# The last batch of an attention and expert kernel, written out for each engine in another order

## The chip, the cores and the metric

One core of a Trainium2 chip runs the kernel. The metric is the device time of one execution in microseconds (us), the median of several runs. The profile lists every instruction of one execution, in us from the first instruction. TensorE has two clock levels, 1.2 and 2.4 GHz; the profile gives the granted clock as a share of the higher one.

## The reference, cut to what matters

For each of four batches of 512 tokens with 128 features: 16-head attention, a layer norm with gamma and beta, a residual and a second layer norm; then a layer that picks 4 of 32 experts for each token, a residual and a third norm.

```python
x = _layernorm(x + _L0_attn_ref(x, Wq, Wk, Wv, rel_table, gamma, beta))   # inside: norm "a"; outside: norm "b"
x = _layernorm(x + _L0_ffn_ref(x, hasher_w, keys, values_down, values_up, scale))          # norm "c"
# _L0_ffn_ref:
h = einsum('btd,pd->btp', x, hasher_w); sim = einsum('btp,np->btn', h, keys)
vals, idx = top_k(sim, 4); w = softmax(vals)
for k in range(4):
    proj = silu(einsum('btd,btdp->btp', x, values_down[idx[..., k]]))
    out = out + einsum('btp,btpd->btd', proj, values_up[idx[..., k]]) * w[..., k:k+1]
return x + out * scale
```

## The kernel before

The kernel runs in rounds `t` of 16 units `u`; each unit has attention scores, exponentials and value products of four heads and a 128-key chunk (`scores`, `exp`, `values`). Round `t` also does the norms, top-4 and first expert layer of batch `t-1`, and the second layer of batch `t-2`. Tables (`JOBS`) say at which unit which small job of TensorE stands; every engine has its own program, written in this order, and semaphores tie them together. After the four attention rounds comes a fifth, `TAIL` (`t == B`), which has no attention, and behind it some lines for the last batch alone. The last batch is `f = B - 1`. A 512-token batch lies as four chunks `c` of 128 tokens.

For that last batch the order of the work is this. The attention output is turned (L1057) and divided on VectorE; `tail_norms` adds the bias, takes statistics and mean (L799, L808), waits for GpSimd to make the inverse root (L432), and scales (L831); gamma, residual and norm "b" follow in the same way. Between them VectorE does the third norm's statistics of batch 2 (`late_y`, L936), whose second-layer products (L1073) run on TensorE meanwhile. `x1` is turned on TensorE, copied by ScalarE to `x1_t`, and the similarities `sim` are made (L1122), copied by ScalarE and searched by VectorE (L885 to L924), with `sdiff` on GpSimd (L550) and the exponential on ScalarE (L728), which also has the tanh of the first layer. The first layer (L1137) makes eight 128x512 products `down0` to `down7`, one for four experts, in three PSUM banks in turn: a bank is free when VectorE's `hidden` (L823) has read it. GpSimd splits the weights in three bf16 parts (L454 to L460), TensorE turns them (`wt`) and ScalarE copies them. `spread_weights` (L1142) then spreads the weights of four experts over a bank of 128x512; VectorE multiplies six of the eight `hid` tiles by it (L967), GpSimd two (L446), from a copy by ScalarE. Only when all eight spreads are done do the eight second-layer products `up0` to `up7` begin (L1073, eight matmuls each in the trace). VectorE adds the residual, takes statistics (L799, L808), GpSimd the inverse root, VectorE scales four chunks (L977), and SyncE stores 256 KB.

PSUM has eight banks: `st_ps` (3), `sm_ps` (2), `ov_ps`, `mi_ps` and `si_ps`. In the attention rounds all have a use; in the tail `st_ps` has the first layer, and `sm_ps`, `ov_ps`, `mi_ps` the spreads.

Of the kernel before, what the change touches and what calls it, by code (L numbers as in the profile page):

```python
# [5 lines left out]
def bass_postln_attention_product_key_ffn(nc, x, w_q, w_k, w_v, rel_table, gamma, beta,  # L6
# [6 lines left out]
    B, S, E = x.shape  # L13
# [4 lines left out]
    J = 4  # L18
# [29 lines left out]
    with ctx:  # L48
# [97 lines left out]
        tail_made, late_step, late_pool = sem("tail_made"), sem("late_step"), sem("late_pool")  # L146
        weighed, tail_weighed = sem("weighed"), sem("tail_weighed")
# [15 lines left out]
        SHORT_JOBS = {**JOBS, 5: ([], []), 6: (["x1t", "shift2"], ["sim", "down0"])}  # L163
        OWN = ("shift0", "shift1", "shift2", "shift3", "o0")
# [26 lines left out]
        def jobs_at(kind, u):  # L191

            return (SHORT_JOBS if kind == SECOND else JOBS).get(u, ([], []))
# [21 lines left out]
        TAIL_VECTOR = [j for j in range(FJ) if j % 3 != 2]  # L215
        TAIL_POOL = [j for j in range(FJ) if j % 3 == 2]

        def hidden_count(f, j):
            return f * FJ + (j + 1)

        def down_bank(t, j):
# [30 lines left out]
        POOL_TAIL, LATE_POOL_TAIL = ["aeps", "apow", "beps", "bpow", "sdiff"], ["ceps", "cpow"]  # L252

        def pool_at(f, name):
            tail = f == B - 1
            if name in LATE_POOL:
                return f * len(LATE_POOL) + ((LATE_POOL_TAIL if tail else LATE_POOL).index(name) + 1)
            return f * len(POOL_STEPS) + ((POOL_TAIL if tail else POOL_STEPS).index(name) + 1)

        def act_at(f, name):  # L260
            return f * len(ACT_STEPS) + (ACT_STEPS.index(name) + 1)
# [22 lines left out]
        def rounds(engine, round_):  # L284

            for t, kind in enumerate(KINDS):
                round_(t, *kind)

# [3 lines left out]
        def _(sp):  # L292
# [96 lines left out]
            store(B - 1)  # L389
            sp.wait_ge(y_stored, 16 * B + 1)  # L390

        @block.gpsimd
        def _(pool):
# [121 lines left out]
            def round_(t, attention, experts, more, late):  # L515
# [11 lines left out]
                if experts and not attention:  # L527
                    norm(f, "a", EPS_ATTENTION, None, None, centre=False)
                    norm(f, "b", EPS_LN, None, None, centre=False)
                    late_norm(t - 2)  # L530
                elif experts:
# [24 lines left out]
                if experts:  # L556
                    split_weights(f)
                    for j in range(FJ // 2) if attention else TAIL_POOL:
# [731 lines left out]
```

## Time and profile before

| | us |
|---|---|
| median of 3 runs (lowest, highest) | 338.67 (338.07, 338.92) |
| the profiled execution's own time | 337.84 |
| its span, first to last instruction | 336.0 |
| TensorE busy in the span | 300.0 |
| last attention output ready in PSUM (end of L1051) | 288.15 |

The last row says where the tail begins: 47.85 us of the span lie behind the last attention product. Outside the span there is 1.84 us. In a row of the timeline the two first numbers are the start and the length, both in us, then come engine, line, operation, what is written and read, shape, how many instructions were merged, and in brackets how long the engine had been idle and what released it. In a row of stretches come start and end, the length, the busy us (and instructions) of TensorE's matmuls, its weight loads, VectorE, ScalarE and GpSimd, the granted clock as a share of 2.4 GHz, the DMA share and GB/s.

### The profile page before, as it was taken

How to read it: one execution, taken by the hardware profiler on the slowest of the kernel's cores; microseconds unless marked ns; L12 is line 12 of the kernel's file. 1: busy time of each engine (PE TensorE's matmuls, PEld its weight loads, DVE VectorE, ACT ScalarE, POOL GpSimd, SP SyncE). 2: the span in 40 equal slices, each digit the busy share in tenths (PEclk: the TensorE clock that was granted, in tenths of full speed). 3: DMA queues.
4: the chain of work that ended last, by engine and by line, in shares of the span. 5: the costliest groups of instructions: out<-in, count | busy, mean ns of one | idle time of the engine just before them, and what ended most of it. 6: DMA issues, size and time to landing. Idle time of an engine off the chain costs nothing. (4 is left out here: it accounts for less than half of the span.)

```text
span 336.0 us, 4908 instructions
## 1 busy us (share of the span) xinstructions
PE 300.0 (89%) x1639; PEld 124.1 (37%) x1639; DVE 235.6 (70%) x514; ACT 200.9 (60%) x392; POOL 126.1 (38%) x208
## 2 busy tenths in 40 slices
PE   4878889999999899999999999999989999837890
PEld 2544322232222233334552433335624232634380
DVE  4448687878879779877659898786598721375533
ACT  2674475776767577787546777884457799202400
POOL 8491700110017502273267212742663237223121
PEclk9999999999999999999999999999999999996797
DMA  5495693099230220102011210120001000001001
GB/s 159 105 271 141 169 295 99 13 324 315 67 72 17 55 57 20 51 21 71 1 36 38 67 40 30 44 60 14 1 0 36 1 1 2 0 0 31 2 0 31
DMA packets 28230, 23.17 MB, mean 69 GB/s; under 512 B 6526, under 2 KB 26670, under 8 KB 28206
## 3 DMA queue, kind: packets, MB, share of 16 engines
q1 hardware_dynamic: 28206, 22.87, 25.0%
q8 instruction: 13, 0.21, 0.3%
q14 instruction: 11, 0.09, 0.1%
HBM read 12.18 MB, written 10.52 MB: 68 GB/s over the span
## 5 line engine op out<-in xcount | busy, mean ns | idle before, releaser
L769 DVE TENSOR_REDUCE neg_max<-sm_ps 128x1 f32<-128x512 f32 x256 | 167.6, 684 | 43.8 <-PE sm_ps L1026 42.9
L668 ACT ACTIVATE probs<-st_ps 128x512 f32<-128x512 f32 x256 | 138.1, 612 | 47.9 <-PE st_ps L1037 47.6
L1026 PE MATMUL sm_ps<-k_stack,q_stack 96*128 96x512 bf16 x256 | 98.1, 384 | 7.7 <-DVE neg_max L769 5.2
L1037 PE MATMUL st_ps<-q_stack,k_stack 128*128 128x512 bf16 x256 | 86.4, 380 | 1.9 <-ACT probs L668 0.8
L1051 PE MATMUL ov_ps<-probs,v_cur 128*32 128x512 f32 x512 | 68.2, 605 | 0.5 <-ACT probs L668 0.5
L1026 PEld LDWEIGHTS sm_ps<-k_stack,q_stack 96*128 96x128 bf16 x256 | 24.6, 96 | 100.7 <-DVE neg_max L769 82.8
L446 POOL TENSOR_TENSOR hid<-hid,w_rows 128x512 f32<-128x512 f32 x26 | 33.1, 1275 | 41.2 <-ACT w_rows L579 34.3
L1037 PEld LDWEIGHTS st_ps<-q_stack,k_stack 128*128 128x128 bf16 x256 | 25.2, 99 | 29.1 <-ACT probs L668 9.3
L1073 PEld LDWEIGHTS si_ps<-up_sb,hid 128*128 128x128 f32 x256 | 30.6, 192 | 1.0
L1073 PE MATMUL si_ps<-up_sb,hid 128*128 128x128 f32 x256 | 31.0, 275 | 0.0
L1137 PE MATMUL mi_ps<-x_t,down_sb 128*128 128x512 f32 x48 | 25.1, 604 | 0.3 <-ACT shift_rows L579 0.3
L823 DVE SCALAR_TENSOR_TENSOR hid<-tanh_sb,mi_ps 128x512 f32<-128x512 f32 x24 | 16.3, 679 | 11.8 <-ACT tanh_sb L705 11.8
L705 ACT ACTIVATE tanh_sb<-mi_ps 128x512 f32<-128x512 f32 x24 | 14.6, 607 | 10.7 <-PE mi_ps L1137 10.7
L418 POOL COPY v_cur<-v_all 128x128 f32<-128x128 f32 x16 | 4.5, 292 | 39.0 <-PE ov_ps L1051 39.0
L1051 PEld LDWEIGHTS ov_ps<-probs,v_cur 128*32 128x32 f32 x512 | 10.1, 108 | 22.3 <-issue 16.8
L402 POOL CAST shift_parts<-neg_max 128x16 bf16<-128x16 f32 x16 | 3.2, 198 | 40.2 <-DVE neg_max L769 30.7
L579 ACT ACTIVATE w_rows<-si_ps 128x512 f32<-128x512 f32 x24 | 15.0, 624 | 2.2 <-PE si_ps L1142 2.2
L1137 PE MATMUL st_ps<-x_t,down_sb 128*128 128x512 f32 x16 | 11.1, 842 | 1.9 <-DVE hid L823 1.9
L427 POOL TENSOR_SCALAR veps<-mv 128x4 f32<-128x4 f32 x8 | 1.8, 227 | 26.8 <-DVE mv L808 19.3
L799 DVE BATCH_NORM_STATS2 stats<-z 128x6 f32<-128x128 f32 x32 | 7.5, 281 | 5.3 <-POOL z L537 5.2
L579 ACT ACTIVATE x_t<-si_ps 128x512 f32<-128x512 f32 x4 | 2.4, 597 | 14.6 <-PE si_ps L1057 14.5
L705 ACT ACTIVATE tanh_sb<-st_ps 128x512 f32<-128x512 f32 x8 | 4.8, 597 | 7.9 <-PE st_ps L1137 7.9
(145 smaller groups left out, 282.2 us busy)
## 6 DMA issues: line engine op xcount, KB each, us to landing
stack_dram<-parts SPq DMA_DIRECT2D x18, 384.0 KB, 4.4
q_stack<-stack_dram SPq DMA_DIRECT2D x16, 288.0 KB
k_stack<-stack_dram SPq DMA_DIRECT2D x16, 288.0 KB
stack_dram<-parts SPq DMA_DIRECT2D x6, 288.0 KB, 4.7
x_sb<-L_attn_x SPq DMA_DIRECT2D x4, 256.0 KB, 3.4
out<-y_out SPq DMA_DIRECT2D x4, 256.0 KB, 2.3
stack_dram<-parts SPq DMA_DIRECT2D x6, 96.0 KB, 2.1
down_sb<-L_ffn_values_down SPq DMA_DIRECT2D x1, 512.0 KB, 7.8
```

The lines of the kernel that those rows point to most:

```text
L446: nc.gpsimd.tensor_tensor(hid[:, j], hid[:, j], w_rows[:, j], ALU.mult).then_inc(weighed, 1)
L579: return nc.scalar.activation(dst, src, ACT.Copy, scale=scale)
L668: nc.scalar.activation(probs[:, u % 2, j, :], st_ps[:, score_bank(u * J + j), :], ACT.Exp, scale=SCORE_SCALE).then_inc(probs_ready, 1)
L705: nc.scalar.activation(tanh_sb[:, j % 3, :], down_bank(t, j), ACT.Tanh, scale=0.5).then_inc(act_step, 1)
L769: nc.vector.tensor_reduce(neg_max[:, g % 2, col:col + 1], sm_ps[:, c % 2, :], AX.X, ALU.max, negate=True).then_inc(max_ready, 1)
L799: i = nc.vector.bn_stats(into[:, c, :], src[:, c, :])
L823: nc.vector.scalar_tensor_tensor(out=hid[:, j], in0=tanh_sb[:, j % 3, :], scalar=1.0, in1=down_bank(t, j), op0=ALU.add, op1=ALU.mult).then ...
L1026: nc.tensor.matmul(sm_ps[:, c % 2, :], q_stack[0:SHIFT_ROW, h, c * P:(c + 1) * P], k_stack[0:SHIFT_ROW, h, :], start=True, stop=True).then ...
L1037: nc.tensor.matmul(st_ps[:, score_bank(k), :], k_stack[:, g * J + j, kc * P:(kc + 1) * P], q_stack[:, g * J + j, :], start=True, stop=True ...
L1051: i = nc.tensor.matmul(ov_ps[j * TILE:(j + 1) * TILE, :], v_cur[:, kc, g * J + j, :], probs[:, u % 2, j, :], start=(g % 2 == 0 and kc == 0 ...
L1073: i = nc.tensor.matmul(si_ps[:, c * P:(c + 1) * P], hid[:, j, c * P:(c + 1) * P], up_sb[:, j, :], start=(j == 0 and c == 0), stop=(j == FJ ...
L1137: i = nc.tensor.matmul(down_bank(t, j), down_sb[:, j * NJ:(j + 1) * NJ, :], x1_t[:], start=True, stop=True)
```

## The change

Everything that the attention rounds do stays, but for two small edits in the last of them. The `TAIL` round and the lines behind it are replaced by an order written out for each engine:

- In the last unit `values` waits for each head's `probs` by itself, no longer for all four. Half of the attention-bias add moves into the last attention round, at unit 10; the other half stays in the tail.
- Norm "a" becomes (z - mean) * gamma, before the inverse root is awaited, and then z * rstd + x, each as four instructions of one chunk. `x1` is signalled chunk by chunk, and each transpose waits for its own.
- The top-4 search reads the similarities in `si_ps`; ScalarE's copy is left out. `sdiff` moves from GpSimd to VectorE, behind `ties`. ScalarE's order is tanh0, exponential, tanh1.
- The first layer has five banks (`st_ps` 3, `sm_ps` 2) and the order 0, 1, 2, 3, 7, 4, 5, 6. Its tanh values go to the eight slots of `probs`. `wt` stands before `down6`.
- Four spreads, then second-layer product 0, and from there spread and product in turn. GpSimd has tiles 2 and 5. The last three products are made first for the chunks 0 and 1 and then for 2 and 3, the halves being in two banks.
- VectorE scales the third norm of batch 2 (before: GpSimd, around 302 us), behind its last weight multiply; the store of batch 2 follows it.
- Residual and statistics of the last norm come in halves. The first half of the output is scaled on VectorE and stored by SyncE, the second scaled on GpSimd and stored from ScalarE's queue, 128 KB each.

The diff, cut to its core:

```diff
@@ tables
+        TAIL_JOBS = {0: (["o1"], [f"up{j}" for j in range(FJ)]), 5: ([], ["x1t"]), 6: (["sim"], []), 11: ([], ["wt"])}
-        TAIL_VECTOR = [j for j in range(FJ) if j % 3 != 2]
-        TAIL_POOL = [j for j in range(FJ) if j % 3 == 2]
+        TAIL_VECTOR, TAIL_POOL = [0, 1, 3, 4, 6, 7], [2, 5]
+        TAIL_DOWN = [0, 1, 2, 3, 7, 4, 5, 6]
+        CHUNKED = 3
-            return st_ps[:, j % 3, :] if t == B else mi_ps[:, :]
+        def tail_down_bank(j):
+            return sm_ps[:, j // 4, :] if j % 4 == 3 else st_ps[:, j % 4, :]
+        def tail_tanh(j):
+            return probs[:, j // J, j % J, :]
+        def tail_y_bank(c, width=S // 2):
+            first = c % 2 * P
+            return (si_ps[:, first:first + width] if c < C // 2 else st_ps[:, 0, first:first + width])
-            return [ov_ps[:, :], sm_ps[:, 0, :], sm_ps[:, 1, :], mi_ps[:, :]][j % 4]
+            return [ov_ps[:, :], mi_ps[:, :], sm_ps[:, 0, :], sm_ps[:, 1, :]][j % 4]
-            for t, kind in enumerate(KINDS):
+            for t, kind in enumerate(KINDS[:-1]):
@@ SyncE
-            store(B - 1)
-            sp.wait_ge(y_stored, 16 * B + 1)
+            store(B - 2)
+            sp.wait_ge(y_made, B)
+            apart(sp)
+            sp.dma_start(half_of(out[B - 1], 0), y_out[:, 0:C // 2]).then_inc(y_stored, 16)
+            sp.wait_ge(y_stored, 16 * (B + 1) + 1)
@@ GpSimd
-            norm(B - 1, "c", EPS_LN, None, None, centre=False)
+            f = B - 1
+            norm(f, "a", EPS_ATTENTION, None, None, centre=False)
+            norm(f, "b", EPS_LN, None, None, centre=False)
+            norm(f - 1, "c", EPS_LN, None, None, centre=False)
+            split_weights(f)
+            for j in TAIL_POOL:
+                weigh(f, B, j)
+            norm(f, "c", EPS_LN, None, None, centre=False)
+            pool.wait_ge(late_pool, pool_at(f, "cpow"))
+            pool.wait_ge(y_stored, f * 16 + 1)
+            for c in SECOND_HALF:
+                i = nc.gpsimd.tensor_scalar(y_out[:, c, :], y[:, c, :], late_mv[:, c, 0:1], late_rstd[:, c:c + 1],
+                                            ALU.subtract, ALU.mult)
+            i.then_inc(half_made, 1)
@@ ScalarE
+            def tail_gate(j):
+                act.wait_ge(tail_down, TAIL_DOWN.index(j) + 1)
+                nc.scalar.activation(tail_tanh(j), tail_down_bank(j), ACT.Tanh, scale=0.5).then_inc(act_step, 1)
+            copy(o_sb[:], ov_ps[:]).then_inc(o_copied, 1)
+            expert_copy(B, "x1t")
+            tail_gate(0)
+            act.wait_ge(side_done, job(B, "sim", is_side))
+            nc.scalar.activation(sexp[:], sdiff[:], ACT.Exp).then_inc(act_step, 1)
...
+            tail_gate(5)
+            expert_copy(B, "wt")
+            tail_gate(6)
...
+            act.wait_ge(half_made, 1)
+            apart(act)
+            nc.scalar.dma_start(half_of(out[B - 1], 1), y_out[:, C // 2:]).then_inc(y_stored, 16)
@@ VectorE
                         if attention and (u, s) == (10, 1):
                             attend(t, 0, t)
+                            if not more:
+                                add_bias(t, slice(0, E // 2))
...
+            f = B - 1
+            attend(f, PAIRS - 1, B)
+            add_bias(f, slice(E // 2, E))
+            dve.wait_ge(tail_made, 2)
+            stats_of(f, "a", z)
+            mv_of(f, "a")
+            dve.wait_ge(dve_step, dve_at(f, "amv"))
+            for c in range(C):
+                i = nc.vector.scalar_tensor_tensor(out=z[:, c, :], in0=z[:, c, :], scalar=mv[:, c, 0:1], in1=gamma_sb[:],
+                                                   op0=ALU.subtract, op1=ALU.mult)
+            i.then_inc(tail_made, 1)
+            dve.wait_ge(tail_made, 3)
+            dve.wait_ge(pool_step, pool_at(f, "apow"))
+            for c in range(C):
+                i = nc.vector.scalar_tensor_tensor(out=z[:, c, :], in0=z[:, c, :], scalar=rstd[:, c:c + 1],
+                                                   in1=x_sb[:, f, c, :], op0=ALU.mult, op1=ALU.add)
...
+            late_y(f - 1, B)
+            late_stats_of(f - 1, B)
+            dve.wait_ge(pool_step, pool_at(f, "bpow"))
+            for c in range(C):
+                nc.vector.tensor_scalar(x1[:, c, :], z[:, c, :], mv[:, c, 0:1], rstd[:, c:c + 1],
+                                        ALU.subtract, ALU.mult).then_inc(tail_normed, 1)
+            mv_of(f - 1, "c")
+            dve.wait_ge(side_ready, job(B, "sim", is_side))
+            found = si_ps[:, 0:C * NE].rearrange("p (c n) -> p c n", c=C)
+            for c in range(C):
+                i = nc.vector.max(top[:, c, :], found[:, c, :])
...
+            nc.vector.tensor_tensor(sdiff[:], found, top[:, :, 0:1].to_broadcast([P, C, NE]), ALU.subtract)                 .then_inc(side_done, 1)
...
+            tail_hidden(7)
+            tail_hidden(4)
+            weigh(0)
+            tail_hidden(5)
+            weigh(1)
+            tail_hidden(6)
+            weigh(3)
+            weigh(4)
+            weigh(6)
+            weigh(7)
...
+            for half, chunks in enumerate((FIRST_HALF, SECOND_HALF)):
+                dve.wait_ge(tail_up, half + 1)
...
-            for c in range(C):
+            for c in FIRST_HALF:
                 i = nc.vector.tensor_scalar(y_out[:, c, :], y[:, c, :], late_mv[:, c, 0:1], late_rstd[:, c:c + 1],
                                             ALU.subtract, ALU.mult)
@@ TensorE
-                pe.wait_ge(probs_ready, J * n + J)
+                last = n == B * U - 1
+                if not last:
+                    pe.wait_ge(probs_ready, J * n + J)
                 for j in range(J):
+                    if last:
+                        pe.wait_ge(probs_ready, J * n + j + 1)
...
+            def tail_up_part(j, c):
+                return nc.tensor.matmul(tail_y_bank(c, P), hid[:, j, c * P:(c + 1) * P], up_sb[:, j, :],
+                                        start=(j == 0 and c % 2 == 0), stop=(j == FJ - 1), skip_group_check=True)
...
                     for c in range(C):
+                        if t == B:
+                            pe.wait_ge(tail_normed, c + 1)
                         i = turn(bank[:, c * P:(c + 1) * P], x1[:, c, :], ident[:])
...
+            tail_first_layer(7)
+            pe.wait_ge(hidden_made, hidden_count(f, 0))
+            tail_first_layer(4)
+            pe.wait_ge(hidden_made, hidden_count(f, 1))
+            tail_first_layer(5)
+            misc(B, "wt", TAIL)
+            pe.wait_ge(hidden_made, hidden_count(f, 2))
+            tail_first_layer(6)
...
-            for j in range(FJ):
-                up(B - 1, j, B + 1)
+            tail_spreading(3)
+            tail_product(0)
+            tail_spreading(4)
+            tail_product(1)
+            tail_spreading(5)
+            tail_product(2)
+            pe.wait_ge(tail_copied, 1)
+            tail_spreading(6)
+            tail_product(3)
+            tail_spreading(7)
+            tail_product(4)
+            for j in range(FJ - CHUNKED, FJ):
+                tail_up_ready(j)
+            for chunks in (FIRST_HALF, SECOND_HALF):
+                for j in range(FJ - CHUNKED, FJ):
+                    for c in chunks:
+                        i = tail_up_part(j, c)
+                i.then_inc(tail_up, 1)
```

## Rows read from the trace of the kernel before

**Rows 1.** The chain that ended last, 290 to 336 us, its sum by line.
```profile
by line: PE st_ps L1137 20.9%; PE si_ps L1073 15.6%; PE si_ps L1122 4.1%; issue 3.1%; DVE hid L967 2.8%; PE si_ps L1057 2.8%; DVE x L831 2.4%; POOLq L48 2.4%; PE sm_ps L1142 2.3%; DVE late_stats L799 1.9%; DVE y_out L977 1.9%; DVE y L936 1.
```

**Rows 2.** Busy time by stretch of us, tail of the kernel.
```profile
297.00:301.00 4.00, 0.00 (x0) 0.00 (x0) 3.65 (x17) 0.00 (x0) 1.25 (x2) 1.00 0.00 0
...
301.00:302.00 1.00, 0.66 (x4) 0.42 (x4) 0.38 (x4) 0.24 (x1) 0.35 (x2) 0.76 0.00 0
...
308.00:309.00 1.00, 1.00 (x2) 0.10 (x1) 0.10 (x1) 0.80 (x2) 0.00 (x0) 0.83 0.00 0
...
311.00:312.00 1.00, 1.00 (x2) 0.27 (x2) 1.00 (x2) 0.00 (x0) 0.86 (x3) 0.88 0.00 0
...
315.00:316.00 1.00, 1.00 (x3) 0.38 (x2) 0.60 (x1) 0.46 (x2) 0.00 (x0) 0.91 0.00 0
```

**Rows 3.** Timeline, norms of the last batch and the turning of x1.
```profile
289.42 7.31 PE L1073 MATMUL si_ps<-up_sb,hid 128*128 128x128 f32 x64
...
293.16 1.04 POOL L432 TENSOR_TENSOR rstd<-veps,minus_half 128x4 f32<-128x4 f32 x1
294.24 1.12 DVE L831 TENSOR_SCALAR z<-z,mv,rstd 128x128 f32<-128x128 f32 x4 [1.58 <-POOL rstd L432]
295.39 0.69 DVE L844 TENSOR_TENSOR z<-z,gamma_sb 128x512 f32<-128x512 f32 x1
...
296.84 0.87 DVE L799 BATCH_NORM_STATS2 stats<-z 128x6 f32<-128x128 f32 x4
...
298.84 0.87 DVE L799 BATCH_NORM_STATS2 late_stats<-y 128x6 f32<-128x128 f32 x4
299.80 1.11 DVE L831 TENSOR_SCALAR x<-z,mv,rstd 128x128 f32<-128x128 f32 x4
...
301.06 0.66 PE L1057 MATMUL si_ps<-ident,x 128*128 128x128 f32 x4 [4.33 <-DVE x L831]
...
301.76 0.60 ACT L579 ACTIVATE x_t<-si_ps 128x512 f32<-128x512 f32 x1 [12.95 <-PE si_ps L1057]
```

**Rows 4.** Timeline, similarities and top-4.
```profile
302.50 1.89 PE L1122 MATMUL si_ps<-sim_w,x_t 128*128 128x32 f32 x8 [0.78 <-ACT x_t L579]
...
304.85 0.47 DVE L885 MAX8 top<-sim 128x8 f32<-128x32 f32 x4 [3.38 <-ACT sim L579]
...
308.90 0.29 DVE L914 TENSOR_TENSOR wexp<-sexp,mask 128x128 f32<-128x128 f32 x1 [1.15 <-ACT sexp L728]
...
310.03 0.29 DVE L924 TENSOR_TENSOR w_tok<-wexp,wscale 128x128 f32<-128x128 f32 x1
```

**Rows 5.** Two instructions by line: lengths in ns, least, median and most.
```profile
L892 DVE TENSOR_TENSOR ties<-sim,top x4: 279/280/496, 123.2 to 305.6; 128x128 f32<-128x128 f32 x4
...
L550 POOL TENSOR_TENSOR sdiff<-sim,top x4: 407/408/512, 121.4 to 305.4; 128x128 f32<-128x128 f32 x4
```

**Rows 6.** Timeline, first layer, weights, spreads and second layer.
```profile
304.20 4.87 PE L1137 MATMUL st_ps<-x_t,down_sb 128*128 128x512 f32 x6
...
311.76 0.43 POOL L460 TENSOR_TENSOR w_parts<-w_res,w_parts 128x128 bf16<-128x128 f32 x1
...
312.95 0.59 ACT L579 ACTIVATE w_t<-si_ps 96x512 bf16<-96x512 bf16 x1
...
316.77 0.60 ACT L705 ACTIVATE tanh_sb<-st_ps 128x512 f32<-128x512 f32 x1 [0.26 <-PE st_ps L1137]
...
317.43 0.38 PE L1142 MATMUL ov_ps<-w_t,spread 96*128 96x512 bf16 x1
...
321.02 7.31 PE L1073 MATMUL si_ps<-up_sb,hid 128*128 128x128 f32 x64
```

**Rows 7.** Timeline, last norm and store.
```profile
328.44 0.69 DVE L936 SCALAR_TENSOR_TENSOR y<-x,si_ps 128x512 f32<-128x512 f32 x1 [5.91 <-PE si_ps L1073]
...
332.13 1.12 DVE L977 TENSOR_SCALAR y_out<-y,late_mv,late_rstd 128x128 f32<-128x128 f32 x4 [1.57 <-POOL late_rstd L432]
333.34 0.38 SPq L386 DMA_DIRECT2D out<-y_out  x1
```

More of the change, by code:

```diff
@@ L526, in round_ @@
                     split_shift(t, 1)
[L527 to L531, printed above, removed]
+                if experts:
                     norm(f, "a", EPS_ATTENTION, z[:], z[:]).then_inc(pool_step, 1)
@@ L557, in round_ @@
                     split_weights(f)
-                    for j in range(FJ // 2) if attention else TAIL_POOL:
+                    for j in range(FJ // 2):
                         weigh(f, t, j)
@@ L880, in expert_steps @@
                     mv_of(f, "b")
-                elif at == ((7, 0) if attention and not late else (6, 3)):
+                elif at == ((6, 3) if late else (7, 0)):
                     dve.wait_ge(side_done, job(t, "sim", is_side))
@@ L925, in expert_steps @@
                                                  ALU.mult))
-                    if not attention:
-                        for j in range(3):
-                            hidden(t, j)
-                if s == 0 and 7 <= u < 7 + FJ and (attention or u >= 10):
+                if s == 0 and 7 <= u < 7 + FJ:
                     hidden(t, u - 7)
@@ L972, in _, with tail_hidden @@
-            mv_of(f, "c")
+            def tail_hidden(j):
+                dve.wait_ge(act_step, act_at(B - 1, f"tanh{j}"))
+                nc.vector.scalar_tensor_tensor(out=hid[:, j], in0=tail_tanh(j), scalar=1.0, in1=tail_down_bank(j),
+                                               op0=ALU.add, op1=ALU.mult).then_inc(hidden_made, 1)
+            f = B - 1
[3 more added lines that the diff above has]
+            stats_of(f, "a", z)
@@ new lines, in _ @@
+            nc.vector.tensor_tensor(sdiff[:], found, top[:, :, 0:1].to_broadcast([P, C, NE]), ALU.subtract)                 .then_inc(side_done, 1)
+            after(f, "above")
+            step(nc.vector.tensor_reduce(n_above[:], above[:], AX.X, ALU.add))
+            after(f, "n_above")
+            for c in range(C):
+                i = nc.vector.tensor_tensor_scan(rank[:, c, :], ties[:, c, :], zeros[:], n_above[:, c:c + 1],
+                                                 ALU.add, ALU.add)
@@ new lines, in _ @@
+            step(i)
+            after(f, "rank")
+            step(nc.vector.scalar_tensor_tensor(out=flat(keep), in0=flat(rank), scalar=float(TOPK),
+                                                in1=flat(ties), op0=ALU.is_le, op1=ALU.mult))
+            after(f, "keep")
+            step(nc.vector.tensor_tensor(mask[:], keep[:], above[:], ALU.add))
+            after(f, "mask")
+            dve.wait_ge(act_step, act_at(f, "sexp"))
+            step(nc.vector.tensor_tensor(wexp[:], sexp[:], mask[:], ALU.mult))
@@ new lines, in _ @@
+            after(f, "wexp")
+            step(nc.vector.tensor_reduce(wsum[:], wexp[:], AX.X, ALU.add))
+            after(f, "wsum")
+            step(nc.vector.reciprocal(winv[:], wsum[:]))
+            after(f, "winv")
+            step(nc.vector.tensor_scalar(wscale[:], winv[:], half_scale[:, 0:1], None, ALU.mult))
+            after(f, "wscale")
+            step(nc.vector.tensor_tensor(w_tok[:], wexp[:], wscale[:].unsqueeze(2).to_broadcast([P, C, NE]), ALU.mult))
+            tail_hidden(0)
@@ L1089, in misc @@
                         pe.wait_ge(side_done, count)
[L1090 removed]
+                else:
                     count = job(t, name, is_kept)
@@ L1227, in round_ @@
                     before, behind = jobs_at(kind, u)
-                    if not attention and u == 0:
-                        before, behind = behind, before
                     todo = maxima_of(t, u, more) if attention else []
```

163 lines of the change are left out of this document (98 added, 65 removed).

## The prediction

> **What bounds the kernel now.** The change touches only what follows the last attention product, so I read the end of the trace. First the chain that ended last [rows 1]: in the last 46 us it runs through TensorE's first layer (L1137, 20.9%) and second layer (L1073, 15.6%), and the rest is a chain of short steps handed from engine to engine. Behind 288.15 no engine is busy throughout; what counts is which wait ends last at each handover. Second the stretches with the granted clock [rows 2]: it is 1.00 until 301.5 (0.76 as the mean of 301 to 302), 0.50 to 308.3, full to 311.8, 0.50 to 315.2, full after. It fell first 4.8 us after TensorE had run out of work at 296.73 [rows 3], and again after the lull that began at 309.07 [rows 6]; it came back 5.8 us after dense work had begun at 302.50 [rows 4], and 3.4 us after the second fall. Third the timeline, step by step [rows 3, 4, 6, 7].
>
> **Part by part, along the path.** The last head's wait changes nothing: the last exponential still ends last.
>
> *Norms, to the start of x1 at 299.80.* Half of the bias add leaves the path. The whole is a 128x512 two-operand instruction like gamma's 0.69 [rows 3]; half saves 0.33. It is done at unit 10 of the last round, where VectorE has no maxima left: free; without that cover it would cost 0.4 once. From the end of the root at 294.20 to the statistics at 296.84 stand 2.64 us: scaling, gamma, residual [rows 3]. Now four instructions come before the end of the root and four behind it; four chunk instructions with scalars took 1.12. If the first four hide wholly behind GpSimd's two steps, 1.5 is saved, and then the third norm of batch 2 sets the pace: its products end at 296.73, residual and statistics take 1.6, and x1 starts at 298.42. But two operands from SBUF meet GpSimd here. `ties` took 496 ns beside `sdiff` and 280 otherwise, and `sdiff` 512 in place of 408 [rows 5]: they held each other up. So I let two of the first four go ahead of GpSimd's steps (0.4 late) and two follow the root (0.6): statistics at 294.20 - 0.33 + 0.40 + 0.60 + 1.2 = 296.1, 0.74 earlier, and x1 as much, at 299.06. The other bound, no holding up, is 0.64 better (298.42).
>
> The Trainium skill (SBUF — State Buffer, section "SBUF: two separate sides") says that VectorE with two SBUF inputs and GpSimd reading SBUF take a shared port pair by turns, each for a whole instruction. The rows on `ties` and `sdiff` agree; by the rule the step gives 0.74, without it 1.38.
>
> *Turning x1.* From its start to the copy's start stand 1.96 us; with a signal per chunk it is the four chunks (1.11), 0.14 of signal and one transpose of about 0.3: 1.57. Saved 0.39; copy at 300.63, similarities from 301.37.
>
> *Similarities and search.* L1122 took 1.89, at the low level [rows 4]. TensorE is idle as early as before and finds little until 301.37, so I let the clock fall as before: no gain; at the full level it would be half, 0.9 better. Without the copy, 0.46 from its end (304.39) to the search becomes 0.10, as between other TensorE ends and VectorE starts (328.33 to 328.44) [rows 4, 6, 7]: saved 0.36. `sdiff` adds 0.2 to VectorE, `ties` loses its 0.2 of delay: nothing. `wexp` waited 1.15 for the exponential [rows 4], which stood behind two tanh. Now it stands behind one: first layer product 0 ends 1.9 after the similarities (303.26), tanh and exponential end at 306.0, the search needs until 306.3: saved 1.15. Sum so far 0.74 + 0.39 + 0.36 + 1.15 = 2.64: `w_tok` ends at 307.68, not 310.32.
>
> *To the first spread.* Before, 7.11 us (310.32 to 317.43) [rows 4, 6]: the first layer stopped for a bank, then fell to the low clock. Five banks take the first five products without a wait, and `hid` 0 and 1 follow `w_tok` by 0.7 and 1.3, before TensorE comes to `down4` and `down5`. So this part is TensorE's: seven products of two passes before `wt`. Six passes took 4.87 at the low level, so about 0.85 each (the last overlaps) [rows 6]; at the full level a product is due each 0.86 (0.26 idle and 0.60 of tanh), 0.43 a pass. The clock I take to come back at 306.4, between the 5.8 after the first dense start (307.2) and the 4.2 after the second (305.6). From 303.26 to 306.4 go 3.7 passes, the other 10.3 take 4.4: 310.8. `wt` 0.45, ScalarE's copy behind tanh5 0.75, signal 0.15: first spread at 312.2. GpSimd's three parts took until 312.19, 1.87 behind `w_tok`; now 309.6, hidden by TensorE. 4.52 in place of 7.11: saved 2.59.
>
> *To the second layer.* Before, all eight spreads came first, 3.59 us (317.43 to 321.02) [rows 6]. Now product 0 needs one spread (0.38), a handover (0.1), one multiply on VectorE (0.68) and a handover: 1.22. Saved 2.37. Queued behind the waits: VectorE's multiply 0 stands behind `hid` 4, whose tanh ends at 310.8: in time.
>
> *Second layer.* 64 matmuls took 7.31. Four spreads come between them (0.38 each at most) and short waits for the multiplies: from nothing to 1.5 and more; I take 1.2, near the upper end since all lie on TensorE's path. VectorE gives a tile each 1.3 us at most (a `hid` and a multiply), TensorE uses one in 0.91 and a spread, and the first ones wait for it; GpSimd's tile 2 is due at 314.1, before product 2. Lost 1.19. End of products at 321.9, not 328.33.
>
> *Last norm and store.* From the last product to the end of scaling 4.92 (333.25) [rows 7]. The first half's residual and statistics lie beside the last six matmuls. Of the second half, the residual is 0.42 for 0.69, statistics and mean 0.71 for 1.25, the scaling 0.85 for 1.12, since the slower of two engines ends it. For GpSimd's chunk the nearest row is 0.43, its part instruction of the same 128x128 [rows 6]: two take the 0.85 that I use; at VectorE's pace it would be 0.3 less, and with the two engines holding each other up as in rows 5 up to 0.6 more. Saved 1.08. VectorE's scaling of batch 2 (1.12) ends before the first half's product; its store has 4 us to land. The store took 2.75 from the end of scaling to the span's end; half the bytes on each of two queues: 0.15 saved. Neither trace nor row shows ScalarE's queue; between nothing gained and 0.4 lost I keep the SyncE row's price.
>
> The Trainium skill (DMA: Bandwidth & Descriptors, section "Issuing engines are not separate DMA queues") says that transfers from different engines run on the same 16 DMA engines and only issue time is saved. No row here shows two; by it the store would save nothing, and the sum would be 0.15 less.
>
> **Sum.** 2.64 + 2.59 + 2.37 - 1.19 + 1.08 + 0.15 = 7.64 us. The span goes from 336.0 to 328.4, the profiled execution's own time from 337.84 to 330.2. The median of the runs shown lies 0.83 above that execution; from 338.67 it gives 331.0, my forecast.
>
> **Rivals.**
>
> 1. *The clock is kinder, or the holding up is absent.* Short pieces of work at 299 to 301 keep the level or bring it back soon: similarities 0.9 shorter, a few passes of the first layer shorter (0.6, then `hid` sets the pace), and 0.64 from the norms. For it: TensorE's lull is shorter by a microsecond than before. Against: a lull of 2 us was enough at 311.8 [rows 2]. Gain 8.6 to 9.9: 329 to 330.
>
> 2. *The clock is as unkind as before.* Back only at 308.2, 6.8 after the fall as at first: 1.8 us at half the speed, 0.9; and a second fall, 3.4 us long as at 311.8, in the second layer with its waits: 1.7. Gain 5.0, with less of it up to 6.6: 332 to 334. For it: two falls before; against: work is denser behind 303.
>
> 3. *Slower: the clock never comes back.* Products now come in pieces between waits for VectorE. All of the first layer and the second at the low level cost 4.5 and 8: gain 7.6 - 12.5, 343.6. It turns to a loss if the low level lasts from 306.4 to about 321.6. Against: both falls ended within 6.8 us under dense work [rows 2].
>
> 4. *The change does not do what it says*: VectorE's strict order makes each product wait, so that the second layer takes 4 more and half the gain goes: 335. The arithmetic above (1.3 against 1.1 a tile, with a lead) speaks against it.
>
> **Chances.** Forecast (gain 6.6 to 8.6) 0.55; rival 1 0.22; rival 2 0.17; rival 4 0.03; rival 3 0.02; no change 0.01. The range takes rivals 1 and 2 but for their ends: gain 5.6 to 9.7, 329.0 to 333.0. About 0.3% is what this measurement can tell from no change; faster 0.97, same 0.01, slower 0.02.
>
> **What would show it.** Right: x1 starts 0.7 to 1.4 earlier; no idle before `wexp`; the five first products of the first layer without a gap; spreads between products; the last product at 320 to 323. The four first gamma instructions show, by their lengths and the root's, whether they held each other up. Wrong: a long wait of VectorE for late tanh, a low clock behind 308, products that wait for multiplies of more than 1 us in sum, or a store from ScalarE that lands over 3 us after scaling.

## The result

| | us |
|---|---|
| after, median of 4 runs (lowest, highest) | 330.58 (330.21, 330.87) |
| before, the runs beside it | 338.37 (337.77, 338.92) |
| ratio, 95% interval | 0.977 (0.975 to 0.979) |
| after, the profiled execution and its span | 330.54, 328.7 |

The forecast was 331.0 (329.0 to 333.0): faster, and 0.4 us off. The span is 7.3 us shorter where the sum said 7.64. To put the executions side by side I count the tail from the start of ScalarE's last copy of the attention output, at 288.21 before and 288.40 after: it is 47.8 us long before and 40.3 after, 7.5 less. The other 0.2 is lost ahead of the tail.

The timeline of the changed kernel from the first norm to the similarities, against [rows 3, 4]:

```profile
292.62 1.14 DVE L1010 SCALAR_TENSOR_TENSOR z<-z,mv,gamma_sb 128x128 f32<-128x128 f32 x4
292.78 0.28 POOL L449 TENSOR_SCALAR veps<-mv 128x4 f32<-128x4 f32 x1 [3.62 <-DVE mv L872]
293.15 1.04 POOL L454 TENSOR_TENSOR rstd<-veps,minus_half 128x4 f32<-128x4 f32 x1
294.30 1.14 DVE L1016 SCALAR_TENSOR_TENSOR z<-z,rstd,x_sb 128x128 f32<-128x128 f32 x4 [0.53 <-POOL rstd L454]
...
295.47 0.87 DVE L863 BATCH_NORM_STATS2 stats<-z 128x6 f32<-128x128 f32 x4
...
296.96 0.69 DVE L961 SCALAR_TENSOR_TENSOR y<-x,si_ps 128x512 f32<-128x512 f32 x1
...
298.47 1.10 DVE L1027 TENSOR_SCALAR x<-z,mv,rstd 128x128 f32<-128x128 f32 x4
298.95 1.15 PE L1190 MATMUL si_ps<-ident,x 128*128 128x128 f32 x4 [2.02 <-DVE x L1027]
...
300.13 0.60 ACT L611 ACTIVATE x_t<-si_ps 128x512 f32<-128x512 f32 x1 [11.13 <-PE si_ps L1190]
...
300.88 1.89 PE L1263 MATMUL si_ps<-sim_w,x_t 128*128 128x32 f32 x8 [0.78 <-ACT x_t L611]
```

x1 starts at 298.47, not 299.80. L1010 is (z - mean) * gamma, L1016 z * rstd + x: the four of L1010 took 1.14 beside GpSimd's root (L454) and the four of L1016 1.14 with GpSimd idle. They did not hold each other up. Two things were ready last before x1, within 0.2 us: the third norm's residual and statistics of batch 2 (L961 at 296.96, as its products end at 296.92; statistics until 298.55), and GpSimd's root of norm "b", which ends at 298.41. By these ends, taking one of the two away would have gained about 0.1 us at most.

The search and the weights, against [rows 4]:

```profile
302.80 0.49 DVE L1034 MAX8 top<-si_ps 128x8 f32<-128x32 f32 x4 [2.95 <-PE si_ps L1263]
...
305.16 0.30 ACT L778 ACTIVATE sexp<-sdiff 128x128 f32<-128x128 f32 x1
...
305.74 0.29 DVE L1055 TENSOR_TENSOR wexp<-sexp,mask 128x128 f32<-128x128 f32 x1
...
306.87 0.29 DVE L1063 TENSOR_TENSOR w_tok<-wexp,wscale 128x128 f32<-128x128 f32 x1
```

No wait is left before `wexp` (305.74); `w_tok` ends at 307.16, not 310.32. First layer, spreads and second layer, against [rows 6]:

```profile
302.58 4.68 PE L1402 MATMUL st_ps<-x_t,down_sb 128*128 128x512 f32 x6
...
307.09 1.88 PE L1402 MATMUL sm_ps<-x_t,down_sb 128*128 128x512 f32 x4
...
308.81 1.88 PE L1402 MATMUL st_ps<-x_t,down_sb 128*128 128x512 f32 x4
...
311.86 0.39 PE L1283 MATMUL ov_ps<-w_t,spread 96*128 96x512 bf16 x1
...
313.11 0.71 PE L1208 MATMUL si_ps<-up_sb,hid 128*128 128x128 f32 x4 [0.21 <-DVE hid L994]
...
320.25 1.50 PE L1208 MATMUL st_ps<-up_sb,hid 128*128 128x128 f32 x12
```

L1402 is the first layer (six passes, then four, then four), L1283 a spread, L1208 the second layer. The first spread starts at 311.86, 5.57 earlier, and the first product 1.25 behind it, not 3.59; the second layer ends at 321.75, not 328.33. The granted clock, against [rows 2]:

```profile
299.00:300.00 1.00, 1.00 (x4) 0.51 (x4) 0.85 (x7) 0.00 (x0) 0.00 (x0) 0.75 0.00 0
300.00:306.00 6.00, 5.22 (x13) 3.22 (x13) 3.02 (x15) 1.40 (x3) 1.27 (x2) 0.50 0.00 0
306.00:307.00 1.00, 1.00 (x3) 0.48 (x2) 0.86 (x5) 0.60 (x1) 0.00 (x0) 0.83 0.00 0
307.00:310.00 3.00, 3.00 (x8) 1.33 (x7) 2.91 (x6) 1.92 (x4) 1.45 (x4) 1.00 0.00 0
```

It fell at 299.5, 2.6 us after the products of batch 2 ended, and came back at 306.3; up to TensorE's last matmul there is no other low stretch. Before there were two, 6.8 and 3.4 us. The end, against [rows 7]:

```profile
321.79 0.42 DVE L1091 SCALAR_TENSOR_TENSOR y<-x,st_ps 128x256 f32<-128x256 f32 x1
...
323.52 1.04 POOL L454 TENSOR_TENSOR late_rstd<-late_veps,minus_half 128x4 f32<-128x4 f32 x1
324.60 0.66 DVE L1106 TENSOR_SCALAR y_out<-y,late_mv,late_rstd 128x128 f32<-128x128 f32 x2 [1.58 <-POOL late_rstd L454]
324.67 1.65 POOL L604 TENSOR_SCALAR y_out<-y,late_mv,late_rstd 128x128 f32<-128x128 f32 x2
325.35 0.38 SPq L411 DMA_DIRECT2D out<-y_out  x1
326.43 0.42 ACTq L792 DMA_DIRECT2D out<-y_out  x1
```

VectorE's two output chunks (L1106) are done at 325.26, GpSimd's two (L604) need 1.65 us and are done at 326.32; the span ends 2.38 later.

### The profile page after: what moved, and what is told of

Read it like the earlier page. It is cut to its first block, busy times and chain, and to the rows that moved or that the text cites. A ratio compares the mean times of both kernels' runs of the same rounds, so it can differ in the third digit from the quotient of the medians.

```text
span 328.7 us, 4916 instructions
## 1 busy us (share of the span) xinstructions
PE 297.9 (91%) x1639; PEld 123.1 (37%) x1639; DVE 237.3 (72%) x521; ACT 200.5 (61%) x391; POOL 125.7 (38%) x207
## 4 chain that ended last, share of the span: by engine, by line
PE 63%; DVE 16%; POOL 6%; ACT 6%; issue 4%; DMA 3%; SPq 1%; POOLq 0%; DVEq 0%
PE sm_ps L1155 15%; PE ov_ps L1184 13%; PE st_ps L1166 11%; DVE neg_max L824 9%; PE mi_ps L1278 5%; PE si_ps L1202 4%; ACT probs L700 3%; PE st_ps L1402 2%; PE si_ps L1190 2%; DMA k_stack<-stack_dram 1%; PE si_ps L1263 1%; DVE stats L863 1%; PE si_ps L1208 1%; PE st_ps L1208 1%; PE si_ps L1283 1%
## 5 line engine op out<-in xcount | busy, mean ns | idle before, releaser
L1166 PEld LDWEIGHTS st_ps<-q_stack,k_stack 128*128 128x128 bf16 x256 | 25.1, 99 | 29.1 <-ACT probs L700 9.3
L1278 PE MATMUL mi_ps<-x_t,down_sb 128*128 128x512 f32 x48 | 25.1, 604 | 0.3 <-ACT shift_rows L611 0.3
L887 DVE SCALAR_TENSOR_TENSOR hid<-tanh_sb,mi_ps 128x512 f32<-128x512 f32 x24 | 16.3, 679 | 11.3 <-ACT tanh_sb L737 11.3
L1202 PEld LDWEIGHTS si_ps<-up_sb,hid 128*128 128x128 f32 x192 | 23.3, 192 | 1.0
L1202 PE MATMUL si_ps<-up_sb,hid 128*128 128x128 f32 x192 | 23.7, 275 | 0.0
L737 ACT ACTIVATE tanh_sb<-mi_ps 128x512 f32<-128x512 f32 x24 | 14.6, 606 | 10.7 <-PE mi_ps L1278 10.7
L1184 PEld LDWEIGHTS ov_ps<-probs,v_cur 128*32 128x32 f32 x512 | 10.2, 108 | 22.1 <-issue 16.8
L449 POOL TENSOR_SCALAR veps<-mv 128x4 f32<-128x4 f32 x8 | 1.9, 237 | 25.1 <-DVE mv L872 17.6
L611 ACT ACTIVATE x_t<-si_ps 128x512 f32<-128x512 f32 x4 | 2.4, 598 | 12.8 <-PE si_ps L1190 12.7
L1278 PEld LDWEIGHTS mi_ps<-x_t,down_sb 128*128 128x128 f32 x48 | 8.3, 190 | 2.9 <-ACT shift_rows L611 1.2
L1283 PE MATMUL si_ps<-w_t,spread 96*128 96x512 bf16 x24 | 9.2, 382 | 0.0
## 6 DMA issues: line engine op xcount, KB each, us to landing
q_stack<-stack_dram SPq DMA_DIRECT2D x16, 288.0 KB
k_stack<-stack_dram SPq DMA_DIRECT2D x16, 288.0 KB
stack_dram<-parts SPq DMA_DIRECT2D x6, 288.0 KB, 4.8
```

Of the source, the lines that this page charges most:

```text
L611: return nc.scalar.activation(dst, src, ACT.Copy, scale=scale)
L737: nc.scalar.activation(tanh_sb[:, j % 3, :], mi_ps[:], ACT.Tanh, scale=0.5).then_inc(act_step, 1)
L887: nc.vector.scalar_tensor_tensor(out=hid[:, j], in0=tanh_sb[:, j % 3, :], scalar=1.0, in1=mi_ps[:], op0=ALU.add, op1=ALU.mult).then_inc(hi ...
L1166: nc.tensor.matmul(st_ps[:, score_bank(k), :], k_stack[:, g * J + j, kc * P:(kc + 1) * P], q_stack[:, g * J + j, :], start=True, stop=True ...
L1184: i = nc.tensor.matmul(ov_ps[j * TILE:(j + 1) * TILE, :], v_cur[:, kc, g * J + j, :], probs[:, u % 2, j, :], start=(g % 2 == 0 and kc == 0 ...
L1202: i = nc.tensor.matmul(si_ps[:, c * P:(c + 1) * P], hid[:, j, c * P:(c + 1) * P], up_sb[:, j, :], start=(j == 0 and c == 0), stop=(j == FJ ...
```

## The experiments

Absolute times of whole kernels are poor witnesses here. The tail began at 288.0 to 288.4 in some executions and at 289.8 to 290.3 in others, of whatever kernel, because TensorE's clock fell once more in the preparation. The five traces with a late tail (three_banks, one_store, pool_beside, before_filler, combo) have a stretch of 3.4 us at the low level between 22 and 27 us, the other eight have none. Here it is in the kernel with one store (the granted clock is the third number from the end):

```profile
22.00:23.00 1.00, 1.00 (x3) 0.15 (x2) 1.00 (x2) 0.00 (x0) 1.00 (x2) 0.66 1.13 367
23.00:24.00 1.00, 1.00 (x3) 0.66 (x2) 0.37 (x2) 0.67 (x2) 1.00 (x5) 0.50 1.00 348
24.00:25.00 1.00, 1.00 (x2) 0.15 (x1) 0.45 (x1) 0.42 (x1) 0.57 (x2) 0.50 0.99 335
25.00:26.00 1.00, 1.00 (x5) 0.68 (x4) 0.11 (x1) 0.53 (x2) 0.65 (x1) 0.63 0.42 135
```

So I read the tail alone, counted from ScalarE's copy, in us:

| kernel | clock low | w_tok ends | first spread | second layer, start to end | last scaling ends | end | whole kernel |
|---|---|---|---|---|---|---|---|
| before | 13.3 to 20.1, 23.6 to 27.0 | 22.1 | 29.2 | 32.8 to 40.1 | 45.0 | 47.8 | 338.37 |
| after | 11.1 to 17.9 | 18.8 | 23.5 | 24.7 to 33.4 | 37.9 | 40.3 | 330.58 (338.37) |
| three_banks | 12.4 to 19.2 | 18.6 | 23.9 | 25.1 to 33.8 | 38.3 | 40.7 | 331.68 (339.47) |
| search_back | 12.8 to 16.2 | 19.2 | 23.0 | 24.3 to 32.9 | 37.5 | 39.8 | 331.85 (339.47) |
| both_back | 11.6 to 18.5 | 20.1 | 25.5 | 26.7 to 35.3 | 39.9 | 42.3 | 332.77 (339.47) |
| spreads_first | 10.7 to 17.6, 27.8 to 31.2 | 18.8 | 23.3 | 27.1 to 36.1 | 40.6 | 43.0 | 333.31 (339.47) |
| filler | never | 17.8 | 21.6 | 22.8 to 31.5 | 36.1 | 38.4 | 328.55 (338.36) |
| vector_scales | 11.3 to 18.2 | 18.7 | 23.5 | 24.8 to 33.4 | 37.4 | 39.8 | 330.12 (338.36) |
| one_store | 12.4 to 19.3 | 18.5 | 24.0 | 25.2 to 33.9 | 37.8 | 40.6 | 330.00 (338.36) |
| pool_alone | 12.8 to 16.2 | 18.1 | 22.3 | 23.6 to 32.2 | 37.5 | 39.9 | 329.66 (338.36) |
| pool_beside | 12.9 to 19.7 | 19.6 | 24.8 | 26.0 to 34.7 | 39.2 | 41.7 | 333.68 (338.84) |
| before_filler | never | 20.5 | 26.2 | 29.8 to 37.1 | 42.0 | 44.8 | 336.47 (338.84) |
| combo | never | 17.8 | 21.6 | 22.8 to 31.5 | 35.4 | 37.8 | 329.19 (338.84) |

Each row is one profiled execution. The last column is the median of the runs of the whole kernel, in brackets that of the kernel before beside it; pool_alone and pool_beside ran once. Low stretches behind the last matmul are left out. The low stretch differs between executions of the same order, so kernels are to be compared where it is alike: vector_scales, one_store and pool_alone have the changed kernel's order up to the last norm, with the stretches 11.3 to 18.2, 12.4 to 19.3 and 12.8 to 16.2.

**Three banks again.**

```diff
-        TAIL_DOWN = [0, 1, 2, 3, 7, 4, 5, 6]
+        TAIL_DOWN = list(range(FJ))
...
-            return sm_ps[:, j // 4, :] if j % 4 == 3 else st_ps[:, j % 4, :]
+            return st_ps[:, j % 3, :]
...
```

> The changed kernel with the first layer of the last batch in three PSUM banks and in its natural order again, all else as changed. If the five banks are what took the lull and the second low clock away, this costs about 2.4 us, the whole of what the stretch from the weights to the first spread gained. Rival: the earlier weights did it. TensorE ends its third product at about 307.3 and the first hid tile is read at 307.75, so it waits only 0.5 us, no low clock follows, and the cost is 0.5 us.

Measured: the end 0.44 us later than in the changed kernel, but under a later low stretch. Beside one_store, which has five banks and the same stretch, the first spread is at 23.9 for 24.0 and the second layer ends at 33.8 for 33.9: under this stretch the banks cost nothing. TensorE had no long wait; its first six products went by as one row:

```profile
303.94 8.07 PE L1402 MATMUL st_ps<-x_t,down_sb 128*128 128x512 f32 x12
```

With the earlier weights the two more banks are not needed here; even the rival's 0.5 us did not appear. But the low stretch ended 1.3 us later than in the changed kernel, so TensorE came later to its fourth product, and `hid` 0 was there. What three banks cost under the earlier stretch was not run.

**The old search.**

```diff
+            nc.gpsimd.tensor_tensor(sdiff[:], sim[:], ...)
...
+            expert_copy(B, "sim")
             tail_gate(0)
-            act.wait_ge(side_done, job(B, "sim", is_side))
+            tail_gate(1)
+            act.wait_ge(half_made, 1)
             nc.scalar.activation(sexp[:], sdiff[:], ACT.Exp).then_inc(act_step, 1)
-            tail_gate(1)
...
-            found = si_ps[:, 0:C * NE].rearrange("p (c n) -> p c n", c=C)
+            found = sim[:]
...
-            nc.vector.tensor_tensor(sdiff[:], found, ...)
```

> The changed kernel with the top-4 search as before: ScalarE copies the similarities, GpSimd makes sdiff, the exponential stands behind tanh1. Five banks stay. If the terms of the prediction's sum add (0.36 + 1.15, and ties held up by 0.2), the end comes 1.5 to 1.7 us later. Rival: TensorE's first layer sets the pace of this stretch, and the search has 0.6 us of slack before it: w_tok about 1.5 later, but the first spread and the end only 0.9 to 1.0 later. In either case ties takes about 0.5 us beside sdiff on GpSimd, where the two held each other up before.

Measured: the tail is 0.46 us shorter than the changed kernel's, not longer, because its low stretch was the short one. Beside pool_alone, with the same stretch, `w_tok` comes 1.1 later, and the first spread and the end of the second layer 0.7 (23.0 for 22.3, 32.9 for 32.2). That is the rival's side (0.9 to 1.0), far from the 1.5 of terms that add. `ties` and `sdiff` again:

```profile
302.75 0.51 POOL L598 TENSOR_TENSOR sdiff<-sim,top 128x128 f32<-128x128 f32 x1 [1.70 <-DVE top L1038]
302.92 0.49 DVE L1043 TENSOR_TENSOR ties<-sim,top 128x128 f32<-128x128 f32 x1
```

Both took half a us, as in [rows 5], and 0.28 for `ties` in the changed kernel.

**Both.**

> Three banks and the old search together. TensorE would stand still from about 307.3 to 309.4. If a lull of 2 us lets the clock fall as in the kernel before, the cost is 2.1 for the lull and 1.7 for a low stretch, 3.8 us in all, far more than the two single costs together (about 1.5). If the clock stays up, 2.1 us.

Measured: 2.0 later than the changed kernel, one low stretch, so 2.1 and not 3.8. The lull was there, and the clock stayed:

```profile
302.18 5.02 PE L1405 MATMUL st_ps<-x_t,down_sb 128*128 128x512 f32 x6
308.95 2.84 PE L1405 MATMUL st_ps<-x_t,down_sb 128*128 128x512 f32 x6 [1.74 <-DVE hid L1003]
```

A lull (a pause of TensorE) of 1.74 us did nothing here; one of 1.90 in the kernel before was followed by a fall. Beside vector_scales, whose stretch is nearly the same (11.3 to 18.2), the first spread is at 25.5 for 23.5 and the second layer ends at 35.3 for 33.4. Banks and search together are worth 1.9, the search alone 0.7, the banks alone nothing. That each covers for the other is likely and not shown, since the three figures come from three different low stretches; even with the rivals' prices, 0.5 and 1.0, the two alone would make 1.5.

**All spreads first.**

```diff
-            tail_product(0)
+            tail_up_ready(0)
             tail_spreading(4)
-            tail_product(1)
+            tail_up_ready(1)
...
+            for j in range(FJ - CHUNKED):
+                tail_product(j)
```

> The changed kernel with all eight spreads ahead of the second layer's first product, the last three products still by halves. By the prediction's terms (2.37 gained at the start, 1.19 lost between the products) this costs 1.2 us. From the changed kernel's trace: spread 7 waits for the multiply of tile 3, which ends at 315.4, so the products start at 315.9 and end at 323.3, 1.5 us later. Rival: the order is neutral, since TensorE has the same work; then 0.3 us or less.

Measured: 2.7 later. From first spread to first product 3.86 for 1.25, that is 2.61; the products take 8.93 for 8.64, although the four spreads are no longer among them, because the clock was low for 3.4 us of them:

```profile
313.72 0.39 PE L1283 MATMUL mi_ps<-w_t,spread 96*128 96x512 bf16 x1 [0.80 <-DVE hid L994]
...
314.92 0.39 PE L1283 MATMUL sm_ps<-w_t,spread 96*128 96x512 bf16 x1 [0.59 <-DVE hid L994]
315.14 0.61 PE L1208 MATMUL si_ps<-up_sb,hid 128*128 128x128 f32 x4
...
316.24 1.06 PE L1208 MATMUL si_ps<-up_sb,hid 128*128 128x128 f32 x4
```

The order costs 1.3 (2.61 less the 1.33 by which the changed kernel's second layer is longer than 7.31), as expected (1.2); the second low stretch, which followed waits for VectorE among the spreads, costs about 1.6. It need not come each time: the fastest run of this kernel, 330.78 us, had a mean clock of 0.990 where the profiled one (332.85) had 0.982, by an estimate 5 us less at the low level.

**Fillers in the lull.**

```diff
+            def filler(n):
+                for _ in range(n):
+                    nc.tensor.matmul(st_ps[:, 1, :], ident_bf[:], k_stack[:, 0, :], start=True, stop=True)
+            filler(8)
             misc(B, "x1t", TAIL)
+            filler(3)
             misc(B, "sim", TAIL)
```

> The changed kernel with 11 more matmuls of no use (128x512 bf16, about 0.22 us each at the full level, result never read): 8 behind the second layer of batch 2, 3 between the turning of x1 and the similarities. They fill most of TensorE's lull from 296.9 to 300.9. If the lull is what makes the clock fall, the clock stays at 1.00, the similarities take 1.0 for 1.89, the first layer's products 0.86 each for 1.7, tanh0 and the exponential come sooner, and the tail from the copy of the attention output to the end is 1.5 to 2.5 us shorter than 40.3. What then bounds it is the search and the hid tiles. Rival: such short work does not count and the fall comes as before; then the tail is the same within 0.3 us, or longer if the fillers run past the chunks of x1.

Measured: 1.9 shorter; 328.55 us against 338.36 for the kernel before on the same chip (ratio 0.973, 0.968 to 0.978). The clock, with lulls filled:

```profile
296.00:300.00 4.00, 3.70 (x21) 2.00 (x20) 3.37 (x18) 0.22 (x1) 1.41 (x3) 1.00 0.00 0
300.00:304.00 4.00, 3.87 (x16) 2.14 (x15) 2.29 (x13) 1.77 (x4) 1.11 (x2) 1.00 0.00 0
```

The similarities took 1.05, for 1.89. The fall in front of the first layer comes from TensorE's lull: with the lull filled it stayed away, here and in the two other kernels with fillers below.

**The same in the kernel before** (18, 3 and 7 fillers ahead of `x1t`, `sim` and `down3`).

> The kernel before with matmuls of no use (128x512 bf16) in TensorE's lulls of the last batch: 18 ahead of the turning of x1, 3 ahead of the similarities, 7 ahead of down3. It tells how much of the old tail was the low clock. Counted from the trace of before: the similarities 0.85 shorter, tanh1 and so the exponential up to 1.1 earlier, no low stretch of 3.4 us in the first layer (1.7): the tail from the copy of the attention output to the end falls from 47.8 to 44.1, and the changed kernel's own gain without the clock is then 44.1 - 38.4 = 5.7 us. Rival: the first low stretch was hidden behind the search, and only the second counts: 46.1.

Measured: 44.8, 3.0 less (3.7 expected), and 336.47 us for 338.84 (0.991, 0.987 to 0.994). Without a low clock the two orders are 44.8 - 38.4 = 6.4 us apart, with it 7.5: about 1.1 us of the change's gain is less time lost to the low clock (3.0 before, 1.9 after), in the executions read.

**The last scaling and the stores.**

```diff
-            pool.wait_ge(late_pool, pool_at(f, "cpow"))
-            pool.wait_ge(y_stored, f * 16 + 1)
-            for c in SECOND_HALF:
-                i = nc.gpsimd.tensor_scalar(y_out[:, c, :], y[:, c, :], late_mv[:, c, 0:1], late_rstd[:, c:c + 1], ...)
-            i.then_inc(half_made, 1)
...
-            for c in FIRST_HALF:
-                i = nc.vector.tensor_scalar(y_out[:, c, :], y[:, c, :], ...)
-            i.then_inc(y_made, 1)
+            for chunks, made in ((FIRST_HALF, y_made), (SECOND_HALF, half_made)):
+                for c in chunks:
+                    i = nc.vector.tensor_scalar(y_out[:, c, :], y[:, c, :], ...)
+                i.then_inc(made, 1)
```

In one_store SyncE besides issues one store of 256 KB when all four chunks are done. In pool_alone the only edit to the changed kernel is that GpSimd waits for VectorE's two chunks (`pool.wait_ge(y_made, B)`).

> The changed kernel with all four output chunks scaled on VectorE, the two stores of 128 KB as changed. GpSimd's two chunks took 1.65 us in the changed kernel and ended 1.06 after VectorE's two. Expected: VectorE's four take 1.12, the last chunk is ready 0.6 us earlier, and the tail is 0.6 us shorter. Rival: the end is set by the first store or by what lies behind both; then nothing is gained.

> All four chunks scaled on VectorE, and one store of 256 KB from SyncE behind the fourth. Against the kernel with two stores it tells what the split and the second queue are worth. In the kernel before the end came 2.75 us behind the last scaling, in the changed one 2.38. Expected: 0.3 to 0.4 us worse than two stores behind the same scaling. Rival: the gain at the end came only from the smaller size of what was left to issue, and with half the bytes issued 0.55 earlier it makes no difference (under 0.1).

> The changed kernel, but GpSimd starts its two output chunks only when VectorE has ended its own two. If the 1.65 us (0.83 a chunk) come from the two engines holding each other up, GpSimd alone needs 0.5 to 0.9 for the two, and the end comes hardly later. If this form of instruction is that slow on GpSimd by itself, it takes 1.65 again, and the end comes about 0.6 us later; VectorE's two then take 0.60 for 0.66 at most.

Measured: with VectorE alone the last scaling ends 3.96 behind the second layer, for 4.57, and the tail is 0.5 shorter (0.6 expected). One store takes 2.79 from there to the end, two take 2.42: the split is worth 0.37, as expected. It is read inside the executions; the medians, 330.00 and 330.12, can't show so little. The transfers themselves, median from issue to landing (the last number), with one store and then with two:

```profile
out<-y_out SPq DMA_DIRECT2D x4, 256.0 KB, 2.3
```

```profile
out<-y_out SPq DMA_DIRECT2D x1, 128.0 KB, 1.9
out<-y_out ACTq DMA_DIRECT2D x1, 128.0 KB, 1.9
```

What is left behind the last scaling is a transfer of 128 KB, which lands in 1.9 us, in place of one of 256 KB, 2.3. That is the size of the gain. With GpSimd behind VectorE:

```profile
323.09 0.60 DVE L1107 TENSOR_SCALAR y_out<-y,late_mv,late_rstd 128x128 f32<-128x128 f32 x2 [1.58 <-POOL late_rstd L454]
...
323.90 1.58 POOL L605 TENSOR_SCALAR y_out<-y,late_mv,late_rstd 128x128 f32<-128x128 f32 x2 [0.85 <-DVE y_out L1107]
```

GpSimd needs 1.58 by itself and 1.65 beside VectorE: this form is slow there by itself, and the two engines together cost 0.07.

**GpSimd beside the norm** (one 128x512 product of unused tiles more).

> The changed kernel with one more instruction on GpSimd, a 128x512 product of two unused SBUF tiles (about 1.27 us), right behind the inverse root of norm a, so that it runs beside VectorE's four instructions z * rstd + x, which read two SBUF tiles each. Those took 1.14 us with GpSimd idle, and the four before them 1.14 beside the inverse root. If any instruction of GpSimd that reads SBUF holds VectorE up for its whole length, the four take 2.2 to 2.4 us and x1 starts about 1 us later. If only the share of time in which GpSimd really reads counts, they take 1.2 to 1.7.

```profile
294.97 1.04 POOL L454 TENSOR_TENSOR rstd<-veps,minus_half 128x4 f32<-128x4 f32 x1
296.09 1.27 POOL L596 TENSOR_TENSOR w_rows<-w_rows 128x512 f32<-128x512 f32 x1
296.12 2.17 DVE L1018 SCALAR_TENSOR_TENSOR z<-z,rstd,x_sb 128x128 f32<-128x128 f32 x4 [0.53 <-POOL rstd L454]
```

The four of VectorE (L1018 here) took 2.17 for 1.14, and x1 started 1.0 later. So this instruction on GpSimd, which reads 512 columns of SBUF, held up VectorE's with two SBUF inputs for 1.03 of its 1.27 us, and the 1.04 us of the root on 4 columns did not (in the changed kernel 0.61 of the 1.14 us of L1010 lay beside it).

**Fillers and VectorE's scaling together.**

> The changed kernel with the 11 fillers and all four output chunks scaled on VectorE. The two act at different places, 1.9 and 0.5 us: tail 37.9 for 40.3 us, the whole about 328.1, and faster than both kernels. Rival: without the low clock the end is set by something else, and they add to less than 2.0.

Measured: tail 37.8; 329.19 us against 338.84 (0.971, 0.967 to 0.974). The two gains add, as expected (37.9). Against the changed kernel (ratio 0.977) the tail is 2.5 us shorter, in one profiled execution of each; the two were not timed side by side.

## Why the prediction was right, and its steps

| step | forecast, us gained | measured |
|---|---|---|
| norms, to x1 | 0.74 | 1.33 |
| turning x1 | 0.39 | 0.30 |
| similarities | 0 | 0 |
| direct read | 0.36 | 0.43 |
| exponential | 1.15 | 1.10 |
| w_tok to the first spread | 2.59 | 2.41 |
| first spread to first product | 2.37 | 2.34 |
| second layer | -1.19 | -1.33 |
| last norm, scaling | 1.08 | 0.35 |
| store | 0.15 | 0.37 |
| sum | 7.64 | 7.30 |

The first row counts from the start of the trace: counted from ScalarE's copy, which came 0.19 later, the norms gained 1.52. The two sums are near each other partly by luck: the norms gave 0.59 more than forecast and the last norm and scaling 0.73 less.

*Norms.* The mechanism was wrong here. Rows 5, two instructions of 128 columns, were carried over to a root of four columns a partition, which held nobody up; the other bound, 298.42, was within 0.05. The Trainium skill's rule (SBUF — State Buffer, section "SBUF: two separate sides") says that GpSimd holds the shared port pair for the whole instruction: the 128x512 product agrees in the main (1.03 us lost beside 1.27), the root does not (1.14 beside it as without it).

*Clock.* Forecast back at 306.4 and one low stretch; it came back at 306.3. That is luck. The forecast counted from the start of dense work, with the fall as late as before (4.8 us behind the end of the products); it fell after 2.6, and the low stretch was again 6.8 us long. Two other executions with the same order up to there came back at 304.3 (pool_alone) and, in a tail that began 1.4 later, at 309.1 (one_store). The second layer ends at 32.2 with the short stretch and at 33.4 to 33.9 with the long one, up to 1.7 us that chance decides, and at 31.5 with fillers and no low stretch. Of rival 1 the part without holding up came true, not the kinder clock; rival 2's second fall did not come in the changed order and did with all spreads first.

*To the first spread.* The working, by TensorE's pace, was right (311.86 for 312.2). But the terms above it are not gains of their own: TensorE had 0.6 us of slack before `down4` (`hid` 0 was made by 307.8, and the weights of `down4` were loaded at 308.4), and the experiments give nothing for the banks, 0.7 for the search, 1.9 for both, each under another low stretch. "The first layer stopped for a bank" was true of the kernel before. But most of the 2.41 is the second low stretch itself: from TensorE's restart behind that stop to the first spread, ten passes and `wt`, the kernel before took 6.46 us (310.97 to 317.43) and both_back, which has the same stop and no fall, 4.67 (308.95 to 313.62). With banks and search both as before the second fall did not come back, so neither is shown to be what took it away; that stays open.

*Last norm and scaling.* The mis-sized term: 0.43 a chunk on GpSimd, from a tensor-tensor row of the same shape, measured 0.79 to 0.83 for `tensor_scalar` with two operands from SBUF. Moving half the scaling to GpSimd lost 0.6 us where it was meant to save 0.27; residual and statistics in halves gained 0.95, for 0.81 forecast.

*Store.* The split was worth 0.37, more than 0.15. The Trainium skill (DMA: Bandwidth & Descriptors, section "Issuing engines are not separate DMA queues") says that all transfers share 16 engines and only issue time is saved. The gain here is of another kind: the last transfer is half as large and lands 0.4 us sooner. It was the same whether the second store was issued 0.53 us behind the first (vector_scales, 325.15 and 325.68) or 1.08 (the changed kernel, 325.35 and 326.43). Two stores from one queue were not tried, so whether the second queue adds anything is not shown.

The last head's own wait moved nothing, as forecast: from the last exponential's end to ScalarE's copy 1.18 us before, 1.13 after.

## What to carry to other kernels

Where a tail hands work from engine to engine, find the pace-setting engine of each stretch first and add up only its work and waits; a fix that another one already covers may be worth nothing by itself, as the two more banks were here. Give the last store as few bytes as you can. Before giving work to GpSimd, take its price from a row of the same form, and look whether VectorE reads two SBUF tiles beside it. When TensorE has a lull of some us in front of dense work, a few matmuls of no use may pay.

## What the runs showed of the hardware

- TensorE's low clock (1.2 GHz) came in stretches of 3.4 or 6.8 us in all thirteen traces, wherever it ended inside the trace, and the same order of work got the one or the other (pool_alone 3.4, one_store 6.8); 8 matmuls of no use (1.89 us) ahead of the turning of x1 and 3 ahead of the similarities kept it at 2.4 GHz up to the last matmul.
- A lull of 1.74 us left the clock up, one of 1.90 in another kernel was followed by a fall. What decides between them stays open.
- The scaling `tensor_scalar` of 128x128 takes 0.79 us on GpSimd and about 0.3 on VectorE (0.60 for two).
- A low stretch of 3.4 us in the preparation (22.3 to 25.7 in one_store) came in five of thirteen traces, whose tails began 1.4 to 2.3 us later than the others'; all edits lie behind it.
- A store of 256 KB took 2.3 us from issue to landing, one of 128 KB 1.8 to 1.9.
- A 128x512 product on GpSimd held up VectorE's instructions with two SBUF inputs for 1.03 of its 1.27 us; an inverse root on 128x4, 1.04 us long, did not.
